# Context loaded transposed from DRAM into two buffers, without transposes on TensorE

## The reference

```
x = L0(x, ctx): h = ln(x); x += causal self-attention(h) ; q = ln(x) Wq, k = ctx Wk, v = ctx Wv ;
                x += cross-attention(q, k, v) ; x += gelu(ln(x) W_fc) W_mproj
x = L1(x, ctx): masked self-attention ; cross-attention with k = ctx ck_w, v = ctx cv_w ; relu feed-forward
x = L2(x, ctx): cross-attention, 16 heads of 16, k = ctx wk, v = ctx wv, mask per element
x = L3(x, ctx): cross-attention, 16 heads of 64, k = ctx w_k (1024 wide), v = ctx w_v (1024 wide)
```

## Time and profile before

| | |
|---|---|
| median of 3 runs | 4481.58 us (4480.01 to 4482.24) |
| the profiled execution | 4480.7 us, its span 4479.0 us |
| PE busy | 4373.1 us, 98% |
| PE weight loads busy | 3533.8 us, 79% |
| DVE busy | 3564.4 us, 80% |
| ACT busy | 2559.6 us, 57% |
| POOL busy | 1380.6 us, 31% |
| DMA | 513.27 MB, mean 115 GB/s |

### The profile page before, as it was taken

The page is one execution under the profiler, slowest core; times in us unless marked ns, Lnnn a source line. Parts: engine busy times, 40 slices in busy tenths (PEclk is TensorE's granted clock), DMA queues, the critical chain, the costliest instruction groups (busy, mean ns, idle before and its releaser), DMA issues. The chain is left out here.

```text
span 4479.0 us, 97142 instructions
## 1 busy us (share of the span) xinstructions
PE 4373.1 (98%) x34368; PEld 3533.8 (79%) x34368; DVE 3564.4 (80%) x10917; ACT 2559.6 (57%) x6849; POOL 1380.6 (31%) x1813
## 2 busy tenths in 40 slices
PE   5999999999999999999999999989999999999998
PEld 4788888888887678787787877778787878888886
DVE  4888888887888888989899898857777777767675
ACT  2565656656565554554545545446666666666665
POOL 3334343434433133333333333221212121212121
PEclk8999999999999999999999999999999999999999
DMA  5554445454445444454544544422222222121211
GB/s 160 151 145 139 146 132 159 129 157 133 145 141 153 132 140 135 120 148 130 151 135 121 149 120 140 142 83 73 64 73 61 76 61 77 58 80 58 79 58 32
DMA packets 393270, 513.27 MB, mean 115 GB/s; under 512 B 109136, under 2 KB 360784, under 8 KB 371280
## 3 DMA queue, kind: packets, MB, share of 16 engines
q1 hardware_dynamic: 385392, 496.82, 38.1%
q10 hardware_dynamic: 7392, 10.24, 0.7%
HBM read 266.30 MB, written 236.72 MB: 112 GB/s over the span
## 5 line engine op out<-in xcount | busy, mean ns | idle before, releaser
L791 ACT ACTIVATE probs_own<-bank 128x384 f32<-128x384 f32 (+2 forms) x1280 | 602.1, 571 | 113.4 <-PE bank L1164 98.3
L1164 PE MATMUL bank<-ht,w_ff 128*128 128x256 f32 x2048 | 489.6, 382 | 1.7 <-ACT ht L689 1.6
L1164 PE MATMUL bank<-w_ff,ffh 128*128 128x256 f32 x2048 | 482.1, 381 | 0.0
L689 ACT ACTIVATE ht<-bank,columns_l 128x256 f32<-128x256 f32 x384 | 196.6, 566 | 476.9 <-PE bank L1224 463.7
L607 POOL TENSOR_SCALAR veps<-meanvar 128x2 f32<-128x2 f32 x256 | 67.9, 265 | 1277.1 <-DVE meanvar L939 1273.8
L856 ACT ACTIVATE probs_other<-bank,negmax 128x120 f32<-128x120 f32 x1024 | 355.6, 375 | 142.9 <-DVE negmax L1144 142.9
L1164 PEld LDWEIGHTS bank<-w_ff,ffh 128*128 128x128 f32 x2048 | 376.8, 190 | 46.0
L1164 PEld LDWEIGHTS bank<-ht,w_ff 128*128 128x128 f32 x2048 | 372.8, 191 | 47.0 <-ACT ht L689 2.5
L1025 DVE TENSOR_REDUCE nmf_other<-bank 128x4 f32<-128x480 f32 x512 | 308.3, 645 | 112.7 <-PE bank L1164 112.5
L1021 DVE CUSTOM_DVE_ANT_0 bank<-bank,mask_rows 128x256 f32<-128x256 f32 x1024 | 392.9, 460 | 6.2 <-PE bank L1164 6.2
L1164 PE MATMUL bank<-kstack_own,qstack_own 96*128 96x256 bf16 (+2 forms) x3072 | 347.8, 245 | 22.1 <-DMA qstack_own<-q_parts 17.8
(11 more groups left out here) (169 smaller groups left out, 10519.7 us busy)
## 6 DMA issues: line engine op xcount, KB each, us to landing
qstack_own<-q_parts SPq DMA_DIRECT2D x96, 768.0 KB, 6.3
kstack_own<-k_parts SPq DMA_DIRECT2D x64, 768.0 KB, 5.7
qstack_other<-q_parts SPq DMA_DIRECT2D x64, 768.0 KB, 6.4
q_parts<-q_parts_own SPq DMA_DIRECT2D x96, 384.0 KB, 2.9
k_parts<-k_parts_own SPq DMA_DIRECT2D x64, 384.0 KB, 2.7
q_parts<-q_parts_own SPq DMA_DIRECT2D x96, 256.0 KB, 2.8
q_parts<-other_parts SPq DMA_DIRECT2D x64, 384.0 KB, 2.6
other_words<-k_parts SPq DMA_DIRECT2D x64, 360.0 KB, 3.7
```

Source lines behind the costliest of these rows:

```text
L689: return nc.scalar.activation(out, in_, ACT.Identity, scale=scale, bias=bias)
L791: nc.scalar.activation(probs[key][0:rows, j % a.slots, 0:n], bank_of(u)[0:rows, 0:n], ACT.Exp, scale=a.scale).then_inc(a_done.sem, 1)
L1164: return nc.tensor.matmul(out, lhsT, rhs, start=first, stop=True, skip_group_check=True)
```

## The change

The host hands the context over by feature (256 x 120 per element), and SP loads it straight into `ct`, which now has two buffers, taken by turns (element modulo 2). The `context` steps on PE and ACT and the tile `c_in` are gone. `load_c` waits for the readers of element e-2. The readers wait for the load's semaphore instead of ACT's. `heads_mul`, a step of DVE, gets a second form for POOL, with waits on its own count; no list names it on POOL. All times of the lists, `START` and `SPREAD` are new; the order of the steps that stay is nearly the same within each pass, and differs in places around the ends of the passes (in `l0`, `norm.2.0` of the last element comes 23 PE steps earlier among the 6,720 that stay, counted without `context`; steps of the first elements of `l1` come later by up to 9).

```
-START = {"l0": 0.0, "l1": 32.06163, "l2": 64.43215}
+START = {"l0": 0.0, "l1": 32.14436, "l2": 64.49674}
...
 l0 PE:
-            scores_exp.own.15/1.38280 scores_exp.own.14/1.40671 probs_v.own.2/1.45284 probs_v.own.3/1.46789 context.c.0/1.52792
-            project_out.own.0/1.57289 project_k.other.0/1.64355 norm.1.0/1.75909 project_q.other.0/1.80928
+            scores_exp.own.15/1.38465 scores_exp.own.14/1.40868 probs_v.own.2/1.45503 probs_v.own.3/1.47015
+            project_out.own.0/1.57077 project_k.other.0/1.64178 norm.1.0/1.75792 project_q.other.0/1.80836
...
 l2 SP:
-            load_c.c.0/0.00000 load_x.x.0/0.99241 load_m.m.0/1.01122 spill_k.own.1/1.12940 spill_k.own.0/1.13881
+            load_c.c.0/0.00000 load_x.x.0/0.97932 load_m.m.0/1.00937 spill_k.own.1/1.11577 spill_k.own.0/1.12514
...
-    def input_of(r, x):
+    def input_of(u, r, x):
-        return (ct, ("context", "c", 0)) if x == "c" else (ht[x], ("turn" if x in r["turned"] else "norm", x, 0))
+        return (ct[:, u.element % 2], c_loaded, ("load_c", "c", 0)) if x == "c" else (ht[x], a_done, ("turn" if x in r["turned"] else "norm", x, 0))
...
             elif kind == "load_c":
-                if w.new(a_full, ("context", "c", 0), 1):
-                    sp.wait_ge(a_full.sem, w.value(a_full, ("context", "c", 0), 1))
-                    settle(sp)
-                sp.dma_start(c_in[:, :], r["ctx"][u.element % NB]).then_inc(c_loaded.sem, 16)
+                for count, tag in passes[max(u.element - 2, 0) // NB]["ct_users"](a_full, d_full):
+                    if w.new(count, tag, 2):
+                        if w.twice:
+                            settle(sp)
+                        sp.wait_ge(count.sem, w.value(count, tag, 2))
+                settle(sp)
+                sp.dma_start(ct[:, u.element % 2, :, :], r["ctx"][u.element % NB]).then_inc(c_loaded.sem, 16)
...
-            elif kind == "context":
-                if w.new(a_full, u.tag):
-                    act_e.wait_ge(a_full.sem, w.value(a_full, u.tag))
-                for count, tag in ahead["ct_users"](a_full, d_full):
...
-                copy(ct[:, :, :], bank_of(u)[:, 0:FT * S2].rearrange("p (f t) -> p f t", f=FT)).then_inc(a_done.sem, 1)
...
-            if kind == "context":
-                if w.new(c_loaded, ("load_c", "c", 0)):
-                    pe.wait_ge(c_loaded.sem, w.value(c_loaded, ("load_c", "c", 0)))
-                bank = take(u)
-                for f in range(FT):
-                    ins = nc.tensor.transpose(bank[:, f * S2:(f + 1) * S2], c_in[:, f * P:(f + 1) * P], ident[0:S2, 0:S2])
-                ins.then_inc(a_full.sem, 1)
...
-    ctx_1024 = ins["ctx_1024"]
+    ctx_1024 = ins["ctx_1024"].rearrange("b (f p) t -> b p f t", p=P)
...
-    sb("c_in", [S2, C])
-    sb("ct", [P, FT, S2])
+    sb("ct", [P, 2, FT, S2])
...
+    inputs["ctx_1024"] = _np.asarray(inputs["ctx_1024"]).reshape(NB, S2, C).swapaxes(1, 2)
```

More of the change, by code:

```diff
@@ L71 @@
[L71 to L75, removed]
@@ L79 @@
+            ff_out.ff.3/4.11221
         """,
         "ACT": """
[L81 to L89, removed]
@@ new lines @@
+            scores_max.other.7/2.26632 scores_max.other.4/2.27949 scores_max.other.0/2.33972 scores_max.other.6/2.38325
+            scores_max.other.5/2.41496 scores_max.other.3/2.42813 negate.other.0/2.45619 negate.other.1/2.46143
+            negate.other.2/2.47815 negate.other.3/2.51552 negate_t.other.0/2.53676 probs_v.other.0/2.75192
+            probs_v.other.1/2.76681 heads_rec.other.0/2.79587 heads_mul.other.0/2.80494 heads_back.other.0/2.82507
+            project_out.other.0/2.89668 stats.2.0/2.91348 norm.2.0/3.14518 ff_in.ff.0/3.46398 ff_in.ff.1/3.57243
@@ new lines @@
+            probs_v.own.1/1.83624 project_v3.three.0/1.84802 project_out.own.0/1.91707 project_v3.three.1/1.95571
+            norm.1.0/2.06896 project_q3.three.1/2.14858 project_q3.three.0/2.18723 scores3.three.2/2.23771
+            scores3.three.3/2.23771 scores3.three.0/2.25645 scores3.three.1/2.25645 turn3.three.3/2.39536
+            project_q3.three.3/2.47995 turn3.three.0/2.52823 project_q3.three.2/2.62127 turn3.three.1/2.68179
+            turn3.three.2/2.71394 scores3.three.4/2.78540 scores3.three.5/2.78540 scores3.three.6/2.88838
@@ new lines @@
+            project_v3.three.0/2.04074 norm.1.0/2.11095 project_q3.three.1/2.19325 project_q3.three.0/2.23189
+            scores3.three.3/2.27916 scores3.three.0/2.30906 scores3.three.2/2.34966 project_v3.three.1/2.39027
+            turn3.three.3/2.41111 project_q3.three.3/2.52462 scores3.three.1/2.53533 turn3.three.0/2.56522
+            project_q3.three.2/2.66593 turn3.three.1/2.69754 turn3.three.2/2.72969 scores3.three.4/2.83348
+            scores3.three.7/2.92984 scores3.three.5/2.95973 scores3.three.6/2.98963 probs_v3.three.0/3.05212
@@ new lines @@
+            negate.own.2/1.60721 negate.own.3/1.61223 negate_t.own.0/1.62823 mask.m.0/1.66856 mask_scores.own.6/1.70524
+            mask_scores.own.4/1.71918 mask_scores.own.3/1.73313 mask_scores.own.7/1.74707 mask_scores.own.5/1.76102
+            mask_scores.own.1/1.77496 mask_scores.own.0/1.78890 mask_scores.own.2/1.80285 probs_v.own.1/1.83160
+            probs_v.own.0/1.85193 heads_rec.own.0/1.86877 heads_mul.own.0/1.87747 heads_back.own.0/1.89677
+            project_out.own.0/1.96174 stats.1.0/1.97785 norm.1.0/2.03474 scores3.three.3/2.26248 scores3.three.2/2.27515
@@ L423, in run @@
     divided = counts("divided", "DVE", ("heads_mul",))
+    divided_by_pool = counts("divided_by_pool", "POOL", ("heads_mul",))
     context_ready = counts("context_ready", "DVE", ("heads_back",))
@@ L653, in _ @@
                                             ALU.add).then_inc(xb_ready.sem, 1)
+            elif kind == "heads_mul":
+                if w.new(recip_ready, ("heads_rec", key, 0)):
+                    g.wait_ge(recip_ready.sem, w.value(recip_ready, ("heads_rec", key, 0)))
+                if w.new(context_ready, ("heads_back", key, 0), 1):
+                    if w.twice:
+                        settle(g)
+                    g.wait_ge(context_ready.sem, w.value(context_ready, ("heads_back", key, 0), 1))
+                for n in range(2):
+                    ins = nc.gpsimd.tensor_tensor(*heads_of(key, n), ALU.mult)
+                ins.then_inc(divided_by_pool.sem, 1)
             elif kind == "mask_probs":
@@ L886, in _ @@
                     reuse(act_e, w, u, divided, [("heads_mul", "other", 0)], u.element - 1)
+                    reuse(act_e, w, u, divided_by_pool, [("heads_mul", "other", 0)], u.element - 1)
                 if w.new(a_full, u.tag):
@@ L987, in _ @@
                     dve.wait_ge(divided.sem, w.value(divided, ("heads_mul", key, 0), 1))
+                if w.new(divided_by_pool, ("heads_mul", key, 0), 1):
+                    dve.wait_ge(divided_by_pool.sem, w.value(divided_by_pool, ("heads_mul", key, 0), 1))
                 if bias is None:
```

242 lines of the change are left out of this document (117 added, 125 removed), and 6 rows, old and new, of the table SPREAD.

## The result

The changed kernel takes 4499.09 us (median of 6 runs, 4493.34 to 4501.56), the kernel before 4481.91 us beside it (6 runs). The ratio is 1.0038, interval 1.0025 to 1.0051: 17 us slower. Forecast were 4464 us and a range that ended at 4472; the forecast was wrong in size and in sign, 35 us too low.

The account below looks back on a forecast made before the run. The prediction took PE (TensorE) to bound the kernel inside every pass. Removed transposes gave 5.4 + 6.7 + 5.4 = 17.5 us, all else 0, so 4480.7 us became 4463.2, as a median 4464; range 4455 to 4472.

Parts of the forecast that it names:

- The reader is to see that inside a pass TensorE waits for nothing: Inside all three passes PE is busy nearly throughout, so removed PE work is worth the time it holds the engine.
- DVE takes over in `l1`: Rival: DVE, 90% busy in `l1`, becomes the limit and the gain of `l1` is lost; 4471 us, chance 0.03.
- The size of the removal: 192 context transposes leave PE, priced by distances of starts: 5.4 us in `l0`, 6.7 in `l1`, 5.4 in `l2`.
- the rival by duration: Rival: each removed PE transpose is worth its 276 ns duration, 53 us in all; 4429 us, chance 0.02.
- The new order: Changed step order: 0 inside the passes, 0 at the seams, with 6 us either way there as likely.
- The seams: PE idle time where `l0` meets `l1` and `l1` meets `l2`, 13.0 and 11.3 us; change taken as 0.
- worse seam: Rival: half of both seams' idle time, 12 us, is added; 4476 us, chance 0.07.
- The load: Context load in 256 runs in place of 120 lands in 3 to 4 us, and nothing waits for it.
- the slower rival: Rival: in `l2` the context load delays the stacks by 2.5 us an element; 4499 us, chance 0.03.
- The sum: Whole kernel: 4480.7 us less 17.5 is 4463.2, for a median 4464 us.

Follow-up runs that it names:

- run 6: Run 5's kernel, with stats.1 of `l0` also moved ahead of ff_mid.ff.0 on DVE; 4484.25 us, ratio 1.0007.
- 15: Run 2's kernel with half of the own heads' division on DVE left out in `l1` (elements 33 to 63), order untouched; 4466.72 us, ratio 0.9962.
- 16: The kernel before, transposes kept, with the same half of the own heads' division left out in `l1`; 4479.57 us, ratio 0.9992.
- 5: Run 2's kernel with DVE's heads_back in `l1` moved ahead of the rest of K's split and the copy of `nm_t_other`; 4487.92 us, ratio 1.0015.
- run 9: Run 2's kernel with the rest of K's split in `l1` moved behind the copy of `nm_t_other` and heads_back on DVE; 4470.39 us, ratio 0.9977.
- run 2: The changed kernel (no context transposes) under the lists, `START` and `SPREAD` of the kernel before, without context steps; 4473.93 us, ratio 0.998.
- run 4: The kernel before with each pair of context transposes done twice (384 in place of 192); 4495.38 us, ratio 1.0029.
- run 1: The changed kernel with loads.first moved from 0.03 to 0.20 in SP's list, so x loads first; 4480.52 us, ratio 0.9993.
- run 3: The kernel before, transposes and context steps kept, under the new times; 4504.42 us, ratio 1.0049.
- 12: Run 2's kernel with only the `START` of `l1` and `l2` set later (32.14436 and 64.51488); 4486.69 us, ratio 1.001.
- 14: Run 1's kernel with only `l1`'s `SPREAD` table of first and last elements put back to the old numbers; 4490.06 us, ratio 1.0019.
- 13: Run 2's kernel with only the feed-forward of `l0`'s last element planned earlier, by the new order's numbers; 4475.44 us, ratio 0.9987.
- run 8: Run 1's kernel with the feed-forward of `l0`'s last element put back to its old, later `SPREAD` numbers; 4490.89 us, ratio 1.0019.

## Why the prediction was wrong, step by step

**"The reader is to see that inside a pass TensorE waits for nothing".** This step failed. A busy share of 99.4 to 99.9% was read as proof of no wait. A wait of some 0.15 us hides within the recorded time of the product before it, and before the change the two chains of DVE ended 0.11 us (`l1`) and 0.13 us (`l0`) ahead of PE, which no view of waits lists. The transposes filled that room. The Trainium skill, "Perfetto Trace Analysis", section "Identifying the Most-Contended Engine", calls the busy share of matmuls a poor measure of how near TensorE is to its roofline, since they are pipelined. The page means pipelined instructions that look smaller than they are; the trace shows another fault of the same measure: 1191 of 1200 us busy with a wait in each element. Cost: `l0` gave 1.6 of 5.4 us and `l1` 1.2 of 6.7, 9 us together (runs 6, 15, 16).

**The rival "DVE takes over in `l1`"** had the right effect and a chance of 0.03. It was set aside since DVE's share would rise by 0.4% only, and "it would have to be a chain". It was a chain, and nothing had been done to look for one. Runs 5, 9 and 15 show it: in each of the three orders tried one of DVE's steps comes late for PE (`ctx_t_own` in 2, the copy in 5, the rest of K's split in 9), and less work on the chain, in the same order, gives the time back. That an element of `l1` gains 0.06 us and no more is shown for these orders, not for all.

**The size of the removal.** Right where PE was the only limit. `l2` gave 0.19 us an element for 0.17 (0.14 in the old order, run 2), `l0` 0.166 in run 6, once DVE's step was moved. The groups behind the removed pairs take 1.95 us in `l0` and 1.99 in `l2`, for 1.94 and 1.99. Run 4 bears out distances of starts as the price (0.21, 0.15, 0.24 us), and the rival by duration (53 us) is out.

**The new order, for which the prediction counts 0 inside the passes and takes 0 at the seams, "and 6 us either way as likely".** The largest failure was that the start wasn't in the sum at all. The term is 15.8 us, in the changed numbers of `SPREAD` for element 0 and visible before any run by sorting SP's list: x behind 18 loads, the last issued at 15.08 us. Runs 1 and 3 show it with and without the removal. Inside the passes 0 was right within 0.08 us an element.

**The seams** took 7.4 and 3.0 us more than before, where about -2 and -1 were forecast from the removal. The bound of 6 us either way was short at the first, and the "worse seam" had a chance of 0.07. The 3.0 of the second is within what two executions of one order differ by there: -0.1 in run 1 for 3.0 in the changed kernel, 2.9 in run 9 for -0.3 in run 2. That PE waits at a seam for a stack's DMA was seen in the changed kernel, 3.46 us:

```profile
1575.87 0.61 PE L1232 MATMUL bank<-ident,x_in 128*128 128x128 f32 x4
1579.94 0.39 PE L1179 MATMUL bank<-qstack_own,kstack_own 99*128 99x256 bf16 x2 [3.46 <-DMA qstack_own<-nm_t_own]
```

My cause for it, `ff_out.3` standing ahead of the turn of the row maxima, fell: in 12 and 14 that inversion stands without a wait over 2 us for this DMA, in 13 it costs little. From 31 to 40, over run 2: feed-forward early 3.2 us, `l1` late 14.5, all new numbers but `l1`'s table 7.0, all new numbers 10.5, these with the feed-forward late 16.3. The later start of `l1` costs, and beside it the early feed-forward gives 5.7 us back (run 8 less run 1). Which of the many short waits at the seam the later start makes stays open. So does why the new numbers cost 10.5 us there without the transposes and 3.7 with them (run 3), and the second seam, where `l1`'s old table cost 14.5 us over run 2 beside the new start.

**The load** was right: nothing waits for it, and in `l2` `load_c` goes out at 3126.29, just behind the end of `project_v3` at 3126.19. The forecast of 3 to 4 us was too high at 2.6, the 512-byte rule of the Trainium skill ("DMA: Bandwidth & Descriptors", "Specifications") showed no cost in this size, and the slower rival built on it did not come about. Its 4499 us is the measured time by chance: from 3120 to 4300 us PE waits for nothing that a view shows, and the elements of `l2` got shorter.

**The sum**, forecast to measured: start 15.8, gain missing in `l0` and `l1` 9.3, seams beside that about 11 (7.4 and 3.0, and the small gain that their elements would have had), less 0.6 for `l2`: 36 us, against the 35 between forecast and median. By run 1 some 3 us of the seams may be this execution's and not the order's.

## What to carry to other kernels

Before an instruction is priced as a gain, find who waits right behind it: compare the end of each input's producer with the start of its reader, take off what passes between the two where the reader waits (0.06 us here), and count what is removed only up to the smallest such room. A busy share can't show that room. In a kernel with a written order, sort the new lists and compare the first steps and the seams of every queue, SP's too.

## What the runs showed of the hardware that was not expected

- 256 runs of 480 bytes landed in 2.6 us, 120 runs of 1 KB in 2.8; SP issued them in 0.39 us and 0.41.
- Two loads of `vectors_l` held SP for 5.60 us, where the other loads took 0.4 to 1.3, and x, issued behind all of them, took 6.8 us to reach its reader (16.42 to 23.20) in place of 2.95.
- The seven distances of starts within the `ctx_t_own` group are 0.05 us longer in sum without the transposes than with them, and 0.10 us shorter in 15 than in 2 (0.05 in 16 than before). In run 4, where the pair is doubled, they are 0.05 shorter than before, which is most of what separates its cost of 0.15 us in `l1` from 0.21. What joins them to DVE's work of that moment was not tried.
